# Attention 2 with a running-minimum pass and later values; the experts of layer 3 written out, the last one's rows by one-hot products

## The reference, cut to what matters

```python
attn = jnp.einsum('bhqd,bhkd->bhqk', q, k)
attn = jax.nn.softmax(attn.astype(jnp.float32), axis=-1)
s = jnp.maximum(jnp.max(attn, axis=-1, keepdims=True) / 255.0, 1e-08)
attn = jnp.clip(jnp.round(attn / s), 0.0, 255.0) * s
out = jnp.einsum('bhqk,bhkd->bhqd', attn, v)
```

```python
h = jax.nn.relu(jnp.einsum('ecd,edf->ecf', dispatched, w1))
expert_out = jnp.einsum('ecf,efd->ecd', h, w2)
out = jnp.einsum('ks,ksm->sm', combine_weights, rerouted)  # rerouted: each token's own rows of expert_out
```

## Time and profile before

| | us |
|---|---|
| median of 3 runs | 1040.38 (1039.15 to 1040.56) |
| the profiled execution: its own time | 1039.42 |
| its span in the trace | 1037.8 |
| PE busy | 708.1 |
| DVE busy | 545.6 |
| ACT busy | 387.3 |
| POOL busy | 332.2 |

### The profile page before, as it was taken

One profiled execution on the slowest core, in us unless ns is written; L12 is line 12 of the kernel. 1 busy time (PEld: TensorE's weight loads), 2 busy tenths in 40 slices (PEclk: granted clock), 3 DMA queues, 4 the chain that ended last, 5 costly groups with the idle time before them and its releaser, 6 DMA issues.

```text
span 1037.8 us, 14236 instructions
## 1 busy us (share of the span) xinstructions
PE 708.1 (68%) x4945; PEld 478.6 (46%) x4990; DVE 545.6 (53%) x1274; ACT 387.3 (37%) x680; POOL 332.2 (32%) x340
## 2 busy tenths in 40 slices
PE   5964759930457777777796793593866059999980
PEld 3433424420444544444563682362455047677660
DVE  2996232246679989898655453827985200000002
ACT  3001023301259989898730233242643031202200
POOL 3821720058306767666505004600000500000005
PEclk9995879975577989887798896696977579999995
DMA  6060226638208989998801627230030131341403
GB/s 196 1 222 16 101 96 213 190 73 81 21 1 152 203 166 188 181 179 167 179 1 71 203 82 235 66 108 0 1 147 16 62 120 50 138 166 43 165 25 121
DMA packets 152028, 115.43 MB, mean 111 GB/s; under 512 B 108908, under 2 KB 138766, under 8 KB 150944
## 3 DMA queue, kind: packets, MB, share of 16 engines
q1 hardware_dynamic: 143256, 93.91, 34.9%
q0 software_dynamic: 7104, 19.42, 7.9%
q10 hardware_dynamic: 1608, 1.32, 0.4%
HBM read 63.98 MB, written 25.46 MB: 86 GB/s over the span
## 4 chain that ended last, share of the span: by engine, by line
PE 29%; issue 9%; DVE 8%; POOL 2%; DMA 2%; ACT 1%; POOLq 0%; SPq 0%; DVEq 0%
PE psum L2088 8%; PE psum L2079 7%; PE psum L1440 3%; PE psum L1715 1%; PE psum L554 1%; PE psum L1455 1%; POOL both L501 1%; DVE both L1969 1%; DVE both L1966 1%; POOL both L1586 1%; PE psum L568 1%; PE psum L1431 1%; PE psum L214 1%; PE psum L1724 1%; PE psum L478 1%
## 5 line engine op out<-in xcount | busy, mean ns | idle before, releaser
L957 POOL TENSOR_SCALAR both<-both 128x1024 f16<-128x1024 f32 x128 | 133.7, 1044 | 99.9 <-ACT both L1123 92.6
L1231 DVE TENSOR_REDUCE both<-psum 128x1 f32<-128x1024 f32 x128 | 155.9, 1218 | 18.7 <-PE psum L1039 18.2
L1123 ACT ACTIVATE both<-psum,both 128x1024 f32<-128x1024 f32 x128 | 153.8, 1215 | 8.9 <-DVE both L1232 6.6
L458 POOL DMA_INDIRECT moe_x_dram<-xn,moe_idx_to x48 | 47.5, 989 | 192.4 <-DVE moe_idx_from L446 178.4
L2116 DVE COPY both<-psum 128x256 f32<-128x256 f32 (+1 forms) x24 | 10.1, 422 | 183.5 <-PE psum L2088 183.5
L1039 PE MATMUL psum<-both 128*128 128x512 bf16 x215 | 80.4, 446 | 37.5 <-ACT both L1123 31.0
L2088 PE MATMUL psum<-both 128*128 128x256 f32 (+1 forms) x384 | 85.5, 381 | 0.0
L1060 PEld LDWEIGHTS psum<-both 128*128 128x128 f16 x1024 | 63.3, 99 | 47.0 <-ACT both L1130 15.8
L1060 PE MATMUL psum<-both 128*128 128x16 f16 x1024 | 69.2, 172 | 19.4 <-DVE xn L1239 7.9
L501 POOL DMA_INDIRECT both<-moe_y_dram,moe_idx_from x48 | 50.4, 1051 | 92.4 <-DMA moe_y_dram<-both 78.4
L2088 PEld LDWEIGHTS psum<-both 128*128 128x128 f32 (+1 forms) x384 | 65.2, 172 | 19.9 <-issue 4.2
(11 more groups left out here) (325 smaller groups left out, 1431.4 us busy)
## 6 DMA issues: line engine op xcount, KB each, us to landing
both<-in_l_experts SPq DMA_DIRECT2D x50, 384.0 KB, 3.7
both<-in_l_experts SPq DMA_DIRECT2D x8, 2048.0 KB, 8.8
grouped_y_dram<-both SPq DMA_DIRECT2D x31, 128.0 KB
grouped_x_dram<-zeros SPq DMA_DIRECT2D x15, 256.0 KB, 2.5
moe_x_dram<-zeros SPq DMA_DIRECT2D x1, 2560.0 KB, 9.1
both<-kpad_dram SPq DMA_DIRECT2D x1, 2048.0 KB, 8.0
both<-grouped_x_dram SPq DMA_DIRECT2D x1, 2048.0 KB, 13.4
both<-moe_x_dram SPq DMA_DIRECT2D x2, 1024.0 KB, 6.7
```

The costliest lines, as they stand in the source:

```text
L458: nc.gpsimd.indirect_dma_start(out=self.x_dram[:, :], out_offset=bass.IndirectOffsetOnAxis(ap=self.idx_to[:, t, k:k + 1], axis=0), in_=xn[ ...
L957: nc.gpsimd.tensor_scalar(r2[n % RSLOTS2], e2[:, n % ESLOTS2, :], 1.0, HALF_BASE, ALU.mult, ALU.add).then_inc(sem("r2_ready"), 1)
L1123: nc.scalar.activation(e2[:, n % ESLOTS2, :], scores_at(n), ACT.Exp, bias=bias2[:, n:n + 1], scale=s2[:, t * H2 + h:t * H2 + h + 1], accum ...
L1231: seq.step(nc.vector.tensor_reduce(nmax2[:, n:n + 1], scores_at(n), AX.X, ALU.max, negate=True))
```

## The change

In attention 2 DVE's reduction and one-column operation become one operation: the scores times the negated scale, written as bfloat16 to a scratch (xnT, two slots, free then), with the minimum over the row accumulated straight into the bias. The factor 255 moves from the exponent to POOL's multiplier and, for the sums, into `scale_out`. Values run seven rounds behind instead of six. Of the PE-turned blocks every second is copied by DVE instead of ACT, four rounds behind.

In layer 3 the expert loop is written out on all engines. Two chunks of the next expert's up products stand ahead of an expert's down products. The weights of an expert come in two DMAs, the up half asked for when the up products two experts back are done. Rows of the last expert no longer go through DRAM: DVE builds from the slot codes three one-hot matrices own7 (128 slots by 1024 tokens, by comparison with a number per partition; the codes are spread over the partitions by a product of ones with a diagonal matrix), ACT copies the last y7, and PE multiplies own7 by y7, 24 products into banks 0 to 3; DVE adds the result to x with the last expert's weight behind all gathered rows, and the gather begins when the first seven experts are stored. The row loads are cut 4, 8, 8 blocks. The output goes out in four quarters. Some semaphores are shared (ring_loaded in place of w5_loaded and w7_loaded).

```diff
                 self.blocks = self.slots // P
-                self.part = 4 * ((self.blocks + 11) // 12)
+                self.parts = (0, 4, 12, 20) if self.blocks > 12 else (0, 4, 8, self.blocks)
...
                 nc.vector.tensor_tensor(self.idx_to[:], self.idx_f, self.spare[:], ALU.add).then_inc(self.sem("idx_ready"), 1)
+                if self.gathered_slots < self.slots:
+                    seq.step(nc.vector.tensor_scalar(self.kept, self.kcode, self.BIG - self.gathered_slots, None, ALU.is_gt))
                 nc.vector.tensor_tensor(self.idx_from[:], self.slot, self.kept, ALU.mult).then_inc(self.sem("idx_ready"), 1)
+                if self.gathered_slots < self.slots:
+                    own_w, own_code = self.last_weight, self.last_code
+                    e = self.gathered_slots // self.C
+                    seq.mark(nc.vector.tensor_copy(own_code, self.code[:, :, e]))
+                    seq.step(nc.vector.tensor_scalar(own_w, self.wkeep[:, :, e], tg[:, self.gate:self.gate + 1], None, ALU.mult))
+                    nc.vector.tensor_tensor(self.diag, bcast(ident[:], 1, NT), bcast(own_code, 2, P), ALU.mult).then_inc(self.sem("diag_ready"), 1)
+                    seq.step(nc.vector.memset(self.wkeep[:, :, e:e + 1], 0.0))
...
-        LAG2, TURN_LAG2, COPY_LAG2 = 6, 4, 3
+        LAG2, TURN_LAG2, COPY_LAG2, VCOPY_LAG2 = 7, 4, 3, 4
...
+        scaled2 = [xnT[:, c, 0:T // 2].bitcast(BF16) for c in range(2)]
...
+        def copied_by_vector(n):
+
+            return turned_by_tensor(n) and n // 4 % 2 == 1
...
-                nc.gpsimd.tensor_scalar(r2[n % RSLOTS2], e2[:, n % ESLOTS2, :], 1.0, HALF_BASE, ALU.mult, ALU.add).then_inc(sem("r2_ready"), 1)
+                nc.gpsimd.tensor_scalar(r2[n % RSLOTS2], e2[:, n % ESLOTS2, :], 255.0, HALF_BASE, ALU.mult, ALU.add).then_inc(sem("r2_ready"), 1)
...
-                if n >= COPY_LAG2 and turned_by_tensor(n - COPY_LAG2):
+                if n >= COPY_LAG2 and turned_by_tensor(n - COPY_LAG2) and not copied_by_vector(n - COPY_LAG2):
...
+                seq.mark(nc.vector.tensor_scalar(ns2[:, some], s2[:, some], -1.0, None, ALU.mult))
...
             def top(n):
                 h, t = n // NT, n % NT
                 dve.wait_ge(sem("scores2_done"), n + 1)
-                seq.step(nc.vector.tensor_reduce(nmax2[:, n:n + 1], scores_at(n), AX.X, ALU.max, negate=True))
-                nc.vector.tensor_scalar(bias2[:, n:n + 1], nmax2[:, n:n + 1], s2[:, t * H2 + h:t * H2 + h + 1], LN255,
-                                        ALU.mult, ALU.add).then_inc(sem("bias2_ready"), 1)
+                if n >= 2:
+                    dve.wait_ge(sem("bias2_ready"), n - 1)
+                nc.vector.tensor_scalar(scaled2[n % 2], scores_at(n), ns2[:, t * H2 + h:t * H2 + h + 1], None,
+                                        ALU.mult, ALU.min, accum_out=bias2[:, n:n + 1]).then_inc(sem("bias2_ready"), 1)
 
             def scale_out(g):
                 dve.wait_ge(sem("e2_ready"), GH2 * NT * (g + 1))
-                seq.step(nc.vector.reciprocal(rz2[:, g * GH2:(g + 1) * GH2, :], zs2[:, g * GH2:(g + 1) * GH2, :]))
+                some = slice(g * GH2, (g + 1) * GH2)
+                seq.step(nc.vector.tensor_scalar(zs2[:, some, :], zs2[:, some, :], 255.0, None, ALU.mult))
+                seq.step(nc.vector.reciprocal(rz2[:, some, :], zs2[:, some, :]))
                 dve.wait_ge(sem("values2_done"), GH2 * NT * (g + 1))
                 nc.vector.tensor_tensor(
                     o2.rearrange("p t (h d) -> p h t d", d=HD2)[:, g * GH2:(g + 1) * GH2],
                     bank[6].rearrange("p (h t d) -> p h t d", h=GH2, t=NT),
                     bcast(rz2[:, g * GH2:(g + 1) * GH2, :], 3, HD2), ALU.mult).then_inc(sem("o2_ready"), 1)
+
+            def copy_T(n):
+                dve.wait_ge(sem("rT2_blocks"), tensor_turns(n + 1))
+                if n >= RSLOTS2:
+                    dve.wait_ge(sem("values2_done"), n - RSLOTS2 + 1)
+                nc.vector.tensor_copy(rT2[n % RSLOTS2], bank[7].bitcast(F16)).then_inc(sem("rT2_copied"), 1)
 
             pair_copied(dve, H2 - 1)
             dve.wait_ge(sem("vi2_ready"), 1)
@@ -1249,6 +1274,11 @@
                 if past > 0 and past % (GH2 * NT) == 0:
                     scale_out(past // (GH2 * NT) - 1)
                 top(n)
+                if n >= VCOPY_LAG2 and copied_by_vector(n - VCOPY_LAG2):
+                    copy_T(n - VCOPY_LAG2)
...
+        own7 = r.f32(3, T)
+        moe7.diag = r.f32(NT, P)
+        moe7.last_code = r.f32(NT)
+        moe7.last_weight = r.f32(NT)
+        own7_code = sb("own7_code", [P, 3])
...
             for i in range(2):
-                sp.dma_start(w7[:, i, :], A["l3_experts"][i]).then_inc(sem(f"w7_loaded{i}"), 16)
+                sp.dma_start(w7[:, i, 0:DC * FF7], A["l3_experts"][i][:, 0:DC * FF7]).then_inc(sem(f"ring_loaded{i}"), 16)
+                sp.dma_start(w7[:, i, DC * FF7:WN7], A["l3_experts"][i][:, DC * FF7:WN7]).then_inc(sem(f"ring_loaded{2 + i}"), 16)
             moe7.load_rows_sync(sp)
-            with sp.Fori(1, E7 // 2) as it:
-                for i in range(2):
-                    sp.wait_ge(sem("down7_done"), (it - 1) * 6 + 3 * i + 3)
-                    sp.dma_start(w7[:, i, :], A["l3_experts"][bass.ds(it * 2 + i, 1)].rearrange("o p n -> p (o n)"))\
-                      .then_inc(sem(f"w7_loaded{i}"), 16)
+            for e in range(2, E7):
+                i = e % 2
+                sp.wait_ge(sem("up7_done"), (e - 1) * FC7)
+                sp.dma_start(w7[:, i, 0:DC * FF7], A["l3_experts"][e][:, 0:DC * FF7]).then_inc(sem(f"ring_loaded{i}"), 16)
+                sp.wait_ge(sem("down7_done"), (e - 1) * 3)
+                sp.dma_start(w7[:, i, DC * FF7:WN7], A["l3_experts"][e][:, DC * FF7:WN7]).then_inc(sem(f"ring_loaded{2 + i}"), 16)
 
...
+            pe.wait_ge(moe7.sem("diag_ready"), 1)
+            pe.wait_ge(sem("small_consts"), 6)
+            for half in range(2):
+                nc.tensor.matmul(bank[6 + half], onesf[:], moe7.diag[:, 4 * half:4 * half + 4, :].rearrange("p t n -> p (t n)"),
+                                 start=True, stop=True).then_inc(sem("codes7_done"), 1)
...
+
+            def up(e, chunks):
+                i = e % 2
+                for f in chunks:
+                    u = e * FC7 + f
+                    if f == 0:
+                        pe.wait_ge(sem(f"ring_loaded{i}"), RING0_LOADS + 16 * (e // 2 + 1))
+                    if u >= 4:
+                        pe.wait_ge(sem("h7_ready"), u - 3)
+                    for c in range(DC):
+                        last = nc.tensor.matmul(bank[f % 4][:, 0:C7], w7[:, i, c * FF7 + f * P:c * FF7 + (f + 1) * P],
+                                                moe7.rowsT[:, c, e * C7:(e + 1) * C7], start=(c == 0), stop=(c == DC - 1))
+                    last.then_inc(sem("up7_done"), 1)
+
+            def down(e, j):
+                i = e % 2
+                lo, n = JT7[j]
+                if j == 0:
+                    pe.wait_ge(sem(f"ring_loaded{2 + i}"), RING0_LOADS + 16 * (e // 2 + 1))
+                    pe.wait_ge(sem("h7_ready"), (e + 1) * FC7)
+                if e:
+                    pe.wait_ge(sem("y7_ready"), 3 * (e - 1) + j + 1)
+                for f in range(FC7):
+                    last = nc.tensor.matmul(bank[4 + j][0:n, 0:D], h7[:, i, f, lo:lo + n],
+                                            w7[:, i, DC * FF7 + f * D:DC * FF7 + (f + 1) * D], start=(f == 0), stop=(f == FC7 - 1))
+                last.then_inc(sem("down7_done"), 1)
+
+            def own_rows(j):
+                pe.wait_ge(sem("y7_last"), j + 1)
+                for t in range(NT):
+                    last = nc.tensor.matmul(bank[t // 2][:, t % 2 * D:(t % 2 + 1) * D], own7[:, j, t * P:(t + 1) * P],
+                                            y7[:, LAST7 % 2, j, :], start=(j == 0 and t % 2 == 0), stop=(j == 2), skip_group_check=True)
+                    if j == 2 and t % 2:
+                        last.then_inc(sem("own7_done"), 1)
+
+            up(0, range(FC7))
+            pe.wait_ge(sem("own7_ready"), 4)
+            for e in range(E7):
+                if e < LAST7:
+                    up(e + 1, range(2))
+                    for j in range(3):
+                        down(e, j)
+                    up(e + 1, range(2, FC7))
+            pe.wait_ge(sem("own7_ready"), 7)
+            down(LAST7, 0)
+            down(LAST7, 1)
+            own_rows(0)
+            down(LAST7, 2)
+            own_rows(1)
+            own_rows(2)
...
-            with act.Fori(0, E7 // 2) as it:
-                for i in range(2):
-                    for f in range(FC7):
-                        act.wait_ge(sem("up7_done"), (it * 2 + i) * FC7 + f + 1)
-                        nc.scalar.activation(h7[:, i, f, :], bank[f % 4][:, 0:C7], ACT.Relu).then_inc(sem("h7_ready"), 1)
+            for e in range(E7):
+                for f in range(FC7):
```

(49 more changed lines are left out.)

70 lines of the change are left out of this document (18 added, 52 removed).

## The result

The changed kernel takes 1008.3 us (median of 4 runs, 1007.2 to 1011.5) against 1039.8 before: a ratio of 0.9708, interval 0.9689 to 0.9728. Forecast were 1010.4. The profiled execution took 1008.82 us with a span of 1007.1.

A forecast was written before the change was run, and what follows sets the result against it. Attention 2 was taken as paced by DVE at 1.385 us a round, ACT close behind, the experts by PE with a 30.5 us tail. Layer 3's -17.5 and attention's -12.5 (-3, -7, -2.5) took 1040.38 to 1010.4 us, range 1001 to 1028.

The forecast's parts named there:

- Seams and store: Layer 3 experts: three inner PE seams of 1.08 us go, -3.2 us; the smaller final store saves 0.8 us.
- The early gather: Layer 3 tail: gather waits for expert 6's store, not 7's, and overlaps PE's last products; 13.8 us of gain.
- Rival D: Layer 3 tail overlaps less, one-hot products running at the 1.2 GHz level: only -8.8 us there, 1019.2 us; chance 0.12.
- The price of the pass: Attention 2: DVE scaling pass with accumulated minimum, read included, taken as 1.26 us, bounds 1.19 and 1.385.
- Rival B: Attention 2: new pass and read cost 1.385 us like the old pair, copy on top: 1024.9 us; chance 0.18.
- The round: Attention 2: DVE stays the bound at 1.36 us a round with copies and 0.01 coupling, against 1.385: -3 us.
- Late rounds: Attention 2: values seven rounds behind recover 7 of 11.2 us lost to late DMA transposes, bounds 0 and 10.
- Rival C: Attention 2: DMA transposes keep the stalls, a longer queue taking what the extra lag gives: 1018.9 us; chance 0.15.
- Boundaries: Attention 2's three group boundaries: ACT's wait and the second late interval shrink, -2.5 us, bounds 0 and -4.
- The row loads: Layer 3 row loads cut 4, 8, 8: earlier first landing against more transposes last; 0 taken, bounds -1.5 and +1.3 us.
- The other side: Rival E, attention 2: accumulating pass takes two cycles an element, round 2.40 us, 1134 us in all; chance 0.05.

The follow-up runs named there:

- through_dram: Changed kernel with the last expert's rows stored and gathered through DRAM like the others, without one-hot products or code products: 1018.5 us, ratio 0.981.
- lag6: Changed kernel with attention 2's values six rounds behind again instead of seven: 1015.0 us, ratio 0.978.
- att_only: Kernel before with only the attention 2 part of the change: 1024.1 us, ratio 0.986.
- parts_8_8_4: Changed kernel with the row loads cut in parts of 8, 8 and 4 blocks as before: 1005.5 us, ratio 0.969.
- combo_dve: Changed kernel with scale_out one pass earlier, row loads cut 8, 8, 4, and all PE-turned blocks copied by DVE: 999.4 us, ratio 0.963.
- dve_copies: Changed kernel with all PE-turned blocks copied by DVE, none by ACT: 1007.3 us, ratio 0.970.

## Why the prediction was right

The time came 2.1 us below the forecast, inside the likeliest case's own range; both stages were forecast by mechanism and place. That the number came so close is in part luck: the two stages gained 32.8 us instead of 30.0, and 2.1 were lost outside them; and in the round, below, two errors of some 7 and 8 us cancelled. By its steps:

**Seams and store**: 3.2 and 0.8 forecast, 4.0 in all; through_dram isolates them with 3.8. **The early gather**: from the first up product on 17.8 were forecast in all, so 13.8 for this part; 15.2 measured. The gather chain took 26.2 us (974.92 to 1001.15) instead of 27.0, since the first gather started 4.0 us behind the last copy's start instead of 5.0; the eight adds took 3.33 (3.5 forecast), and PE ended at 1003.59, 0.9 before DVE, in the order forecast. One wait was left out of the sum: the last down products stand directly behind the last up products and wait 0.76 us for ACT's Relu, which cost nothing, as DVE's queue ended last. Rival D fell: the clock stayed at 1.00.

**The price of the pass**: 1.26 taken, bounds 1.19 and 1.385; it is 1.205. I had counted the accumulator read as a small instruction of its own; on DVE it hides under the next pass. Rival B, to which I gave 0.18, fell. The Trainium skill (VectorE: DVE Perf Modes, Two Vector instructions with no wait between them) is right that there are two instructions, as the rows show; that the second costs time doesn't follow. The section The DRAIN you can't avoid, from which the prediction took that the pipe empties behind each operation, also says that a next operation that isn't held starts earlier, and the rows agree: the next pass starts 0.08 us before the shown end of the one before.

**The round**: 1.36 forecast. In an undisturbed stretch eight rounds take six intervals of 1.207 and two of 1.81, 10.86 us, so 1.357: right, by two errors that cancel. The pass was 0.055 too dear, and the coupling term of 0.01 too small: I let ACT's copy be absorbed, as ACT has room on average, but it holds the score slot, and through three slots DVE loses 0.6 us to it, as much as to its own copy. With the right pass and that absorption DVE's floor would have been (8 x 1.205 + 0.61) / 8 = 1.28, so ACT's 1.29 would have decided and the forecast been 8 to 9 us too fast. The round is right by luck: this is the step of the prediction whose mechanism was incomplete. That also is why the split of the copies gives little (1 to 3 us), which I had not priced by itself. The step from 1.385 gives 127 x 0.028 = 3.6 us (forecast 3).

**Late rounds**: 7 forecast, bounds 0 and 10. What is left over the pace outside the boundaries, 183.6 - 127 x 1.357 - 8.9 = 2.4 us, was 11.2: 8.8 gained. Only some 5.2 of them are the distance's (lag6, without its boundaries). The rest is not taken apart; at least in part it is a matter of where a loss is entered, as the pace of 1.357 holds what ACT's copies cost and the floor of 1.385 did not, though ACT needed 1.405. So the 7 us forecast for the distance were somewhat too many. Rival C, that the transposes keep up the stalls, fell, though the DMA share rose to 1.00 and the median landing from 3.3 to 3.5 us.

**Boundaries**: 2.5 forecast, 1.4 measured (10.3 to 8.9 over the pace). Of the terms of the sum this one is off most in proportion. I forecast that the second late interval would shrink, and it went; but the first one grew from 4.09 to 4.45, 3.93 and 4.63 us at the three boundaries: the wait for the values stayed, and the scaling by 255, priced at 0.2, took 0.50, 0.17 and 0.69 there. The interval follows the scaling one to one: with 0.17 or 0.18 it is mostly 4.10 to 4.13 in att_only, parts_8_8_4 and through_dram too, with 0.48 it is 4.43, with 0.80 it is 4.74. In sum 3.6 + 8.8 + 1.4 = 13.8 (forecast 12.5).

**The row loads**: 0 taken, bounds -1.5 and +1.3; it is 0 to +0.8, by the clock.

**The other side**, E: no part of it; the pass takes 1.205 us for its 1024 elements, the reduction of that shape 1.215.

## What to carry to other kernels

In a ring of few slots, price a piece of work that blocks one engine as lost on all of them: here a copy cost every eight rounds 0.6 us whether on the engine with room or on the one without, and moving work from one to the other bought little. That holds where the two go at nearly the same pace (exponentials 1.18 us apart, passes 1.205). When a consumer empties a bank that a producer waits for, queue the emptying while a finished piece of the producer's next work is still in store; one line moved so gave 5 us here, more than the rebalancing of copies did. And a last, late transfer can be worth replacing by products on the busiest engine: 24 products, some 10.8 us of TensorE (the last 16 take 7.17), bought 15. A sum of waits names a suspect but is no price: PE's values waited 12.9 us for the transposes before the change and 13.9 in combo_dve, and DVE then waited 18.2 us for scores in the one and 3.7 in the other.

## What of the hardware was not expected

- A DVE pass with accumulator output (1.280 us) lets the next one start 1.205 us after its own start, its read (0.083 us) included; the plain reduction of the same shape (1.215 us) with its dependent one-column operation took 1.385.
- The same small DVE operation (the scaling by 255, 128x32, SBUF to SBUF) takes 0.17 to 0.18 us or up to 0.88. It stands 44 times in the eleven profiles of kernels that have it. Seven times it is long: 0.50 and 0.69 in the changed kernel, 0.80 in att_only, 0.48 in parts_8_8_4, 0.88, 0.63 and 0.74 in dve_copies. Each of these seven ends 0.03 to 0.04 us after the instruction on which POOL (L972 in the changed kernel, 1.05 us) was when it started. The other 37 met POOL idle, in its last 0.14 us, or starting behind them. That is what waiting for the end of POOL's instruction looks like; no run took POOL's work away to prove it. The Trainium skill (SBUF — State Buffer, Who interferes with whom) has `tensor_scalar` among the operations that can hold the pair of ports that VectorE shares with GpSimd, where one then waits for the other; the 44 durations agree.
- The granted clock rose from 0.50 to 1.00 3.5 to 3.9 us after the first of PE's forty row transposes where they ran on without a pause (five profiles), and 8.6 to 9.0 us after it where PE paused 1.0 to 1.3 us behind the first eight (seven profiles). They took 7.7 to 7.8 us in the one case and 10.0 to 10.3 in the other.
- Profiled executions that share the program up to attention 2 reach it between 306.8 and 311.8 us, and combo_dve's profiled execution took 995.6 us where its median is 999.4: differences of 4 to 5 us in the whole time of one execution say nothing about a change of one stage.
